# Constant products ahead of a convolution's small matmuls: a head of 128x512 and one of 128x96 before every fourth channel

## The chip, the core and the metric

The kernel runs on one core of a Trainium2 chip. The engines of that core are TensorE (PE in the rows, its weight loads PEld), VectorE (DVE), ScalarE (ACT), GpSimd (POOL) and SyncE (SP, which issues DMAs). The metric is the device time of one execution in microseconds (us), as the median of several runs. Lower is better.

## The reference

Two transformer layers run on `x` of 64 sequences by 64 positions by 128 channels, with a context of 96 channels: a cross attention, a mixture of experts, a second cross attention and a second mixture of experts, each added to `x`. Only one step of the first layer matters here. After the first attention, each of the 128 channels is convolved causally over its 64 positions with its own kernel `K` (made by an FFT in the reference), and the result is scaled and shifted:

```python
Kf = jnp.fft.rfft(K, n=n, axis=-1)
xf = jnp.fft.rfft(x, n=n, axis=1)
y = jnp.fft.irfft(xf * Kf.T[None], n=n, axis=1)[:, :L]
return y + x * D_skip
...
y = y * (1.0 + mod_gate * scale_out) + mod_gate * shift_out
xt = x_text + y
```

## The kernel before, in words

The program is a row of phases, each with its own block in which every engine has a list of instructions; at a block's end all engines meet. The phases that matter are `first_attention`, `convolution` and `first_mlp_and_router`, in this order. All data is fp32, and each fp32 matmul of the program stands in the trace as two weight loads and two matmul records.

In `convolution` a channel's convolution is a product with a 64 by 64 Toeplitz matrix. The 4096 tokens lie as 128 partitions by 32 tiles, with two sequences in a tile, one on partitions 0 to 63 and one on 64 to 127. So a channel takes two matmuls (`b2` = 0, 1), each with a 64x64 stationary matrix (`G.toe`) and 32 moving columns (`G.XM`); the two stand in opposite corners of the 128x128 array, on rows 0 to 63 and columns 0 to 63, and on rows 64 to 127 and columns 64 to 127. 16 channels (`CH`) make a group, of which there are 8 (`NG`), and a group fills one of four PSUM tiles `psy`.

The order is set by the lists and by semaphores. TensorE goes through all groups, and waits only for a PSUM tile to come free, three groups back (`y_film`). VectorE takes a finished group out of PSUM with the scale (`ym`, L1045) and adds the shift (`yn`, L1051), and GpSimd adds it to `G.XT` (L1025). SyncE loads the weights of the next phase meanwhile. ScalarE has nothing to do.

Two more constants appear in the change. `G.ones` is a 128x128 matrix of ones, and `G.pen` (128 partitions by 32 tiles by 64) holds the first attention's mask penalties, which are all zero for the masks of this case. Both are complete before the convolution begins.

Other lines that are used as measures below: in the first attention L825 (97 rows by 128 stationary columns, 512 moving), L829, L833, L834 (full or nearly full arrays, 128 moving), the weight folding's L281 and L293 (128x128 stationary) and L283 and L294 (16x128 stationary), which alternate; in the second attention L1825 and L1826 (128 stationary columns), L1831 (96x64 stationary, two side by side), L1793 (128x128 stationary, 8 moving columns) and L1863 (128x32 stationary). In the phase behind the convolution L1224 is its first transpose and L1230 its first product, both with 128x128 stationary.

Of the kernel before, what the change touches and what calls it, by code (L numbers as in the profile page):

```python
# [15 lines left out]
P = 128  # L16
B, T, D = 64, 64, 128
# [161 lines left out]
def after(eng, sem, n):  # L179

    if not isinstance(n, int) or n > 0:
        eng.wait_ge(sem, n)
# [810 lines left out]
def convolution(nc, C, A, G):  # L993


    CH = 16
    NG = D // CH
    with ExitStack() as ctx:
        psy = [C.ps(f"psy{j}", [P, CH, NT], ctx) for j in range(4)]
        ym = [C.sb(f"ym{j}", [P, NT, CH], ctx=ctx) for j in range(2)]  # L1000
        yn = [C.sb(f"yn{j}", [P, NT, CH], ctx=ctx) for j in range(2)]
        s = {n: C.sem("conv_" + n) for n in ("y", "y_film", "y_shift", "y_sum", "padded", "weights")}
        with nc.Block() as block:

            @block.sync
            def _(sp):
                sp.wait_ge(s["padded"], 1)
                m = G.mlp
                loads = ((m["w1"][:], A["L0_xattn_W1"]), (m["w2"][:], A["L0_xattn_W2"].rearrange("(c p) d -> p c d", p=P)),
                         (m["b2"][:], A["L0_xattn_b2"].partition_broadcast(P)),  # L1010
                         (m["gout"][:], A["L0_xattn_g_norm_out"].partition_broadcast(P)),
                         (m["bout"][:], A["L0_xattn_b_norm_out"].partition_broadcast(P)),
                         (m["rw1"][:], A["L0_ffn_rw1"]), (m["rw2"][:, :, 0:NE], A["L0_ffn_rw2"].rearrange("(c p) e -> p c e", p=P)),
                         (m["rb2"][:], A["L0_ffn_rb2"].partition_broadcast(P)))
                for dst, src in loads:
                    sp.dma_start(dst, src).then_inc(s["weights"], 16)
                sp.wait_ge(s["weights"], 16 * len(loads))

            @block.gpsimd
            def _(pool):  # L1020
                pool.memset(G.mlp["rw2"][:], 0.0).then_inc(s["padded"], 1)
                for g in range(NG):
                    ch = slice(g * CH, g * CH + CH)
                    pool.wait_ge(s["y_shift"], g + 1)
                    pool.tensor_tensor(G.XT[:, :, ch], G.XT[:, :, ch], yn[g % 2][:], ALU.add).then_inc(s["y_sum"], 1)  # L1025
                    pool.wait_ge(s["y_sum"], g + 1)

            @block.tensor
            def _(pe):
                for g in range(NG):  # L1030
                    after(pe, s["y_film"], g - 3)
                    for c in range(CH):
                        for b2 in range(2):
                            rows = slice(T * b2, T * b2 + T)
                            mm = pe.matmul(psy[g % 4][rows, c, :], G.toe[rows, g * CH + c, :], G.XM[rows, :, g * CH + c],
                                           start=True, stop=True)
                    mm.then_inc(s["y"], 1)

            @block.vector
            def _(dve):  # L1040
                for g in range(NG + 1):
                    if g < NG:
                        dve.wait_ge(s["y"], g + 1)
                        after(dve, s["y_shift"], g - 1)
                        dve.tensor_tensor(ym[g % 2][:], psy[g % 4][:].rearrange("p c b -> p b c"),  # L1045
                                          G.FO[:, :, g * CH:g * CH + CH], ALU.mult).then_inc(s["y_film"], 1)
                    if g > 0:
                        q = g - 1
                        dve.wait_ge(s["y_film"], q + 1)
                        after(dve, s["y_sum"], q - 1)  # L1050
                        dve.tensor_tensor(yn[q % 2][:], ym[q % 2][:], G.FO[:, :, D + q * CH:D + q * CH + CH],  # L1051
                                          ALU.add).then_inc(s["y_shift"], 1)
# [1429 lines left out]
def program(nc, A, out, last=99):  # L2482
    with ExitStack() as ctx:
# [25 lines left out]
        with ExitStack() as early:  # L2509
            G.XM = C.sb("XM", [P, NT, D], ctx=early)  # L2510
            G.FO = C.sb("FO", [P, NT, 256], ctx=early)
            G.pen = C.sb("pen", [P, NT, T], ctx=early)
            G.gin = C.sb("gin", [P, D], ctx=early)
            G.bin = C.sb("bin", [P, D], ctx=early)
            G.wq = C.sb("wq", [P, P], ctx=early)
            G.wk = C.sb("wk", [DC, P], ctx=early)
            G.wv = C.sb("wv", [DC, D], ctx=early)
            G.filmw = C.sb("filmw", [DC + 1, 512], ctx=early)
            G.toe = C.sb("toe", [P, D, T], ctx=early)
            with ExitStack() as first:  # L2520
                G.dskip, G.sign = C.sb("dskip", [P, 8], ctx=first), C.sb("sign", [P, 1], ctx=first)
                G.at0 = {n: [C.sb(f"{n}{j}", k, ctx=first) for j in range(2)] for n, k in (
                    ("kb", [P, 2, H0, T]), ("abd", [P, P]), ("at", [P, P]), ("us", [DC + 1, P]))}
                G.ring = [C.sb(f"cs{j}", [P, DC], ctx=first) for j in range(RING)]
                G.norm = {"mv": G.FO[:, NT - 5, 0:2 * NT].rearrange("p (t k) -> p t k", k=2),
                          "rstd": G.FO[:, NT - 5, 2 * NT:3 * NT], "shift": G.FO[:, NT - 5, 3 * NT:4 * NT]}
                G.kernel, G.fold = Kernel(G), Fold(C, A, G, first)
                setup(nc, C, A, G)
                C.end_phase()
                if last >= 1:  # L2530
                    first_attention(nc, C, A, G)
                    C.end_phase()
            if last >= 2:
                convolution(nc, C, A, G)
                C.end_phase()
# [49 lines left out]
```

## Time and profile before

| What | Value |
|---|---|
| Median of 3 runs | 938.84 us (936.86 to 939.61) |
| Span of the profiled execution | 935.4 us, 3.4 us under that median; what lies around the span is not in the profile |
| TensorE busy, share of the span | 710.3 us, 76% |
| VectorE busy | 673.2 us, 72% |
| Mean granted TensorE clock over the span | 0.80 of 2.4 GHz |
| The convolution's matmuls | 512 records, 259.7 to 287.3 us of the span |

A share of the span is an average over phases with different limits, so the rows of the one phase that is changed count here. The granted clock is given as a share: 1.00 is 2.4 GHz and 0.50 is 1.2 GHz. Ends of matmul records are modelled, and records overlap, so the distance between starts tells how fast TensorE goes, not the length of a record.

### The profile page before, as it was taken

The page shows a single profiled execution, that of the slowest core. Times are in us where ns is not written, and L with a number is a line of the kernel's source. Part 1 is how long each engine was busy: PE and PEld are TensorE (multiplying, and loading weights), DVE is VectorE, ACT ScalarE, POOL GpSimd, SP SyncE. Part 2 cuts the span into 40 slices and gives each one's busy share as a digit, 9 for nine tenths or more (in the row PEclk, how much of TensorE's full clock was granted, in tenths as well). Part 3 has the DMA queues.
Part 4 walks back from the last instruction along what each step waited for, and adds up shares of the span by engine and source line. Part 5 has one row for each costly group of instructions (what it writes and reads, how often), then busy time and mean ns, then how long its engine had stood idle before and what let it go on. Part 6 is the DMA issues. An engine that isn't in the chain of part 4 may idle for free. (4 is left out here: it accounts for less than half of the span.)

```text
span 935.4 us, 20537 instructions
## 1 busy us (share of the span) xinstructions
PE 710.3 (76%) x6072; PEld 508.4 (54%) x6072; DVE 673.2 (72%) x3212; ACT 473.4 (51%) x1318; POOL 564.8 (60%) x931
## 2 busy tenths in 40 slices
PE   0686898979883999972498528998888874799970
PEld 0353554545483656631275426766666652699970
DVE  6898989978524688769111167598998887699974
ACT  3566576735200455450133175577777761577740
POOL 7688877766526544210677667345777767277770
PEclk9767787957555999996599855798988885899995
DMA  6300112997213977700365330000000002698928
GB/s 143 57 25 10 41 45 64 86 88 96 40 45 140 290 250 257 243 23 0 39 115 132 88 137 1 2 4 13 25 26 25 25 28 76 216 279 264 260 69 270
DMA packets 98829, 94.41 MB, mean 101 GB/s; under 512 B 37511, under 2 KB 82302, under 8 KB 98142
## 3 DMA queue, kind: packets, MB, share of 16 engines
q1 hardware_dynamic: 91268, 79.34, 33.1%
q0 software_dynamic: 6592, 13.58, 6.0%
q8 instruction: 50, 0.82, 0.4%
q14 instruction: 61, 0.50, 0.3%
q10 hardware_dynamic: 858, 0.17, 0.1%
HBM read 47.76 MB, written 43.19 MB: 97 GB/s over the span
## 5 line engine op out<-in xcount | busy, mean ns | idle before, releaser
L2402 POOL DMA_INDIRECT expert_pairs<-e_ys,e_home x78 | 75.4, 967 | 38.4 <-issue 23.5
L1742 POOL TENSOR_SCALAR a_kb<-a_kr,a_m,a_bk 128x128 f32<-128x128 f32 x128 | 57.9, 452 | 44.4 <-ACT a_kr L1981 32.3
L1760 POOL DMA_INDIRECT expert_slots<-r_rows,r_slotu x64 | 63.3, 989 | 30.3 <-DVE r_rows L2136 15.1
L950 DVE MATCH_REPLACE8 work<-m,work 128x64 f32<-128x64 f32 x384 | 75.7, 207 | 0.0
L1484 POOL DMA_INDIRECT ex_rows<-rows,slot_source x32 | 30.7, 960 | 52.7 <-POOLq L1163 43.2
L937 DVE MAX8 m<-work 128x8 f32<-128x64 f32 x384 | 57.0, 209 | 0.0
L825 PE MATMUL psf<-filmw,us 97*128 97x512 f32 x64 | 51.6, 902 | 3.0 <-ACT FO L846 2.9
L1815 PE MATMUL a_pss<-a_kb,a_qt 32*64 32x256 f32 x512 | 41.5, 463 | 13.9 <-ACT a_pp L1966 11.7
L2168 DVE TENSOR_REDUCE a_mx<-a_pss 128x8 f32<-128x512 f32 x64 | 43.9, 686 | 8.1 <-PE a_pss L1815 7.8
L2369 PE MATMUL e_ps<-e_XH,e_wh 128*128 128x256 f32 x156 | 48.1, 308 | 1.5 <-DVE e_XL L2414 1.5
L1536 ACT ACTIVATE ex_hs<-ex_psh,vec 128x512 f32<-128x512 f32 x32 | 22.0, 687 | 51.2 <-PE ex_psh L1517 50.5
L2371 PE MATMUL e_ps<-e_XH,e_wl 128*128 128x256 f32 x156 | 44.6, 286 | 0.0
L2370 PE MATMUL e_ps<-e_XL,e_wh 128*128 128x256 f32 x156 | 44.6, 286 | 0.0
L1961 ACT ACTIVATE a_pp<-a_dd 128x512 f32<-128x512 f32 x32 | 20.2, 631 | 45.1 <-DVE a_dd L2177 45.1
L1890 PE MATMUL a_psp<-ident,a_pp 128*128 128x128 f32 x256 | 39.5, 306 | 1.9 <-ACT a_pt L2014 1.9
L2219 DVE RECIPROCAL a_rt<-a_pso 128x128 f32<-128x128 f32 x31 | 29.5, 951 | 14.8 <-PE a_pso L1882 11.9
L1309 ACT ACTIVATE rt_rs<-mlp_psh,vec 128x512 f32<-128x512 f32 x32 | 22.0, 687 | 34.7 <-PE mlp_psh L1267 34.7
L203 POOL TENSOR_SCALAR mlp_ln_v<-mlp_ln_mv 128x4 f32<-128x4 f32 x24 | 5.5, 229 | 54.0 <-DVE mlp_ln_mv L195 54.0
L1494 POOL DMA_INDIRECT planes<-ex_ys,slot_home x32 | 31.2, 976 | 10.9 <-issue 9.1
L2177 DVE TENSOR_TENSOR a_dd<-a_mx,a_pss 128x512 f32<-128x512 f32 x64 | 35.5, 554 | 2.2
L808 PE MATMUL pss<-kb,qt 128*64 128x256 f32 x128 | 28.9, 541 | 10.7 <-ACT kb L846 10.7
L2014 ACT ACTIVATE a_pt<-a_psp 128x512 f32<-128x512 f32 x64 | 35.4, 611 | 2.2 <-PE a_psp L1890 2.0
(464 smaller groups left out, 2418.2 us busy)
## 6 DMA issues: line engine op xcount, KB each, us to landing
expert_slots<-rt_unfilled SPq DMA_DIRECT2D x151, 130.0 KB, 2.6
ahead<-folded_weights SPq DMA_DIRECT2D x20, 386.0 KB
e_wf<-folded_weights SPq DMA_DIRECT2D x19, 386.0 KB, 4.2
planes<-rt_zeros SPq DMA_DIRECT2D x4, 1024.0 KB
ew<-in_L_ffn_ew SPq DMA_DIRECT2D x16, 256.0 KB, 4.0
pair_y<-expert_pairs SPq DMA_DIRECT2D x16, 256.0 KB, 5.6
e_xr<-expert_slots SPq DMA_DIRECT2D x27, 130.0 KB, 3.3
folded_weights<-fold_done SPq DMA_DIRECT2D x8, 384.0 KB, 4.3
```

Source lines behind the costliest of these rows:

```text
L825: pe.matmul(psf[:], us[j][:], G.filmw[:], start=True, stop=True).then_inc(s["film"], 1)
L937: mx = dve.max(m8[x.j][:, h, r, :], src[:, h, :])
L950: return own.did(dve.match_replace(wk_[x.j][:, h, :], m8[x.j][:, h, r, :], src[:, h, :], TAKEN))
L1742: m = pool.tensor_scalar(kb[a.j][:, :, h, :], k, m4[:, h:h + 1], bk4[:, h:h + 1], ALU.mult, ALU.add)
L1760: pool.indirect_dma_start(G.slots, bass.IndirectOffsetOnAxis(ap=slot[:, b, k, t:t + 1], axis=0), rb[b % NB][:, k, t, :], None).then_inc(se ...
L1815: mm = pe.matmul(pss[half][T * b:T * b + T, h, 0:HG * T], qt[g.j][rows, T * b:T * b + T], kb[g.j][rows, b, :, :], start=True, stop=True)
L1890: mm = pe.transpose(psp[half][:, k, :], pp[x.j][:, h:h + 2, :].rearrange("p h k -> p (h k)"), G.ident[:])
L2168: dve.tensor_reduce(m, scores(half), AX.X, ALU.min).then_inc(s["lowest"], 1)
L2369: pe.matmul(psh[m][c][:], wh[j][:, m, c, :], XH[j][:], start=True, stop=False)
L2370: pe.matmul(psh[m][c][:], wh[j][:, m, c, :], XL[j][:], start=False, stop=False)
L2371: pe.matmul(psh[m][c][:], wl[j][:, m, c, :], XH[j][:], start=False, stop=True).then_inc(h_ps[m][c], 1)
L2402: pool.indirect_dma_start(G.pair, bass.IndirectOffsetOnAxis(ap=home[i % NY][:, k:k + 1], axis=0), ys[i % NY][:, k, :], None).then_inc(kept ...
```

## The change

TensorE's list of `convolution` gets one matmul of 512 columns at its start, and one of 96 columns ahead of every fourth channel, 32 of them in all. Each has `G.ones` as stationary matrix (128x128) and the first columns of `G.pen` as moving ones, and writes a PSUM tile of its own, `psw`, that nothing reads. They have no semaphore, neither to wait for nor to raise. No instruction of another engine changes.

```diff
@@ -997,6 +997,8 @@
     NG = D // CH
     with ExitStack() as ctx:
         psy = [C.ps(f"psy{j}", [P, CH, NT], ctx) for j in range(4)]
+        psw = C.ps("conv_warm", [P, 512], ctx)
+        held = G.pen[:, 0:512 // T, :].rearrange("p n t -> p (n t)")
         ym = [C.sb(f"ym{j}", [P, NT, CH], ctx=ctx) for j in range(2)]
@@ -1027,9 +1029,12 @@
 
             @block.tensor
             def _(pe):
+                pe.matmul(psw[:], G.ones[:], held, start=True, stop=True)
                 for g in range(NG):
                     after(pe, s["y_film"], g - 3)
                     for c in range(CH):
+                        if c % 4 == 0:
+                            pe.matmul(psw[:, 0:96], G.ones[:], held[:, 0:96], start=True, stop=True)
                         for b2 in range(2):
                             rows = slice(T * b2, T * b2 + T)
                             mm = pe.matmul(psy[g % 4][rows, c, :], G.toe[rows, g * CH + c, :], G.XM[rows, :, g * CH + c],
```

TensorE's list at the seam of the first attention and the convolution, before (an x counts equal instructions of the program, out<-in are tiles, and the shape is that of the result):

```order
L825 MATMUL psf<-filmw,us 128x512
L637 UNCONDITIONAL_BRANCH
L1028 UNCONDITIONAL_BRANCH
L1035 MATMUL psy<-XM,toe 64x32 x256
L1003 UNCONDITIONAL_BRANCH
```

All 256 matmuls of the convolution stood in one run of one shape. The same place in the changed list (`conv_warm` is `psw`; the line numbers are those of the changed kernel):

```order
L825 MATMUL psf<-filmw,us 128x512
L637 UNCONDITIONAL_BRANCH
L1030 UNCONDITIONAL_BRANCH
L1032 MATMUL conv_warm<-pen,ones 128x512
L1037 MATMUL conv_warm<-pen,ones 128x96
L1040 MATMUL psy<-XM,toe 64x32 x8
```

The last two rows then repeat to the end of the phase, 32 times in all: one product over the full array, then eight on its quarters.

## Rows read from the trace of the kernel before

**Rows 1.** Groups of instructions, 259 to 293 us: count | busy us, mean ns | idle before, releaser

```profile
L1035 PE MATMUL psy<-XM,toe 64*64 64x32 f32 x512 | 27.5, 291 | 2.3 <-PEq L637 2.3
L1035 PEld LDWEIGHTS psy<-XM,toe 64*64 64x64 f32 x512 | 27.4, 223 | 3.9 <-issue 3.9
...
L1045 DVE TENSOR_TENSOR ym<-psy,FO 128x512 f32<-128x512 f32 x8 | 5.5, 692 | 30.0 <-PE psy L1035 30.0
```

**Rows 2.** Timeline at the convolution's end: start us, us, instruction, idle before and releaser

```profile
287.29 0.69 DVE L1045 TENSOR_TENSOR ym<-psy,FO 128x512 f32<-128x512 f32 x1 [2.12 <-PE psy L1035]
287.90 1.28 DVE L1051 TENSOR_TENSOR yn<-ym,FO 128x512 f32<-128x512 f32 x2
288.73 2.89 POOL L1025 TENSOR_TENSOR XT<-XT,yn 128x512 f32<-128x512 f32 x2 [2.16 <-DVE yn L1051]
292.09 1.28 ACT L1289 ACT_TABLE_LOAD   x1 [34.01 <-PEq L1003]
```

**Rows 3.** TensorE by stretch: stretch, its length, busy us, granted clock, DMA share, GB/s

```profile
259.70:287.30 27.60, 27.52 (x512) 0.50 0.15 39
...
292.10:303.60 11.50, 1.11 (x4) 0.50 0.65 273
303.60:307.00 3.40, 3.38 (x7) 0.50 0.98 396
307.00:310.00 3.00, 3.00 (x14) 1.00 1.07 315
229.00:237.00 8.00, 8.00 (x26) 0.50 0.95 113
221.90:225.00 3.10, 3.10 (x17) 1.00 0.43 48
586.00:592.00 6.00, 6.00 (x57) 0.50 0.00 0
602.00:605.00 3.00, 3.00 (x64) 1.00 0.02 5
```

**Rows 4.** TensorE's timeline, 228 to 237 us

```profile
228.72 1.06 PE L825 MATMUL psf<-filmw,us 97*128 97x512 f32 x1
229.58 0.64 PE L829 MATMUL psb<-abd,cs 128*96 128x128 f32 x2
230.00 0.63 PE L833 MATMUL psa<-xf,wq 128*128 128x128 f32 x2
230.43 0.63 PE L834 MATMUL psa<-cf,wk 96*128 96x128 f32 x2
...
231.46 0.79 PE L283 MATMUL side<-fold_bt,fold_ar 16*128 16x128 f32 x2
232.18 0.80 PE L281 MATMUL side<-ident,fold_wr 128*128 128x128 f32 x2
232.91 0.79 PE L283 MATMUL side<-fold_bt,fold_ar 16*128 16x128 f32 x2
```

**Rows 5.** TensorE's timeline, 588 to 592 us

```profile
588.03 0.80 PE L1825 MATMUL a_psx<-XF,a_wq 128*128 128x128 f32 x2
588.62 0.63 PE L1826 MATMUL a_psx<-ctxT,a_wk 96*128 96x128 f32 x2
589.18 0.70 PE L1831 MATMUL a_psx<-a_wv,ctxT 96*64 96x64 f32 x8
589.81 1.88 PE L1793 MATMUL a_pso<-e_wgt,XF 128*128 128x8 f32 x8
591.61 0.66 PE L1863 MATMUL a_pso<-a_pt,a_vb 128*32 128x64 f32 x16
```

**Rows 6.** TensorE's timeline, 222 to 225 us, at the full clock

```profile
222.06 0.49 PE L293 MATMUL side<-ident,fold_w2r 128*128 128x128 f32 x2
222.47 0.48 PE L294 MATMUL side<-fold_bt,fold_a 16*128 16x128 f32 x2
...
224.01 1.02 PE L825 MATMUL psf<-filmw,us 97*128 97x512 f32 x2
224.87 0.38 PE L829 MATMUL psb<-abd,cs 128*96 128x128 f32 x2
```

**Rows 7.** TensorE's timeline, 603 to 604 us, at the full clock

```profile
603.08 0.45 PE L1831 MATMUL a_psx<-a_wv,ctxT 96*64 96x64 f32 x8
603.46 1.06 PE L1793 MATMUL a_pso<-e_wgt,XF 128*128 128x8 f32 x8
```

**Rows 8.** TensorE's timeline behind the convolution

```profile
303.62 1.11 PE L1224 MATMUL mlp_pst<-ident,mlp_xs 128*128 128x128 f32 x4 [3.93 <-DVE mlp_xs L211]
304.52 4.83 PE L1230 MATMUL mlp_psh<-mlp_xf,mlp_w 128*128 128x512 f32 x8
```

## The prediction, as it was put on record

> **What bounds the kernel now.** I read the groups of instructions in the convolution first, then the end of that phase in the timeline, then the table by stretch for the clock, and last those places where TensorE changes between shapes. The first view shows who waits. VectorE was idle for 30.0 us ahead of its eight evictions, each time for TensorE, and TensorE's 512 records wait for nothing but the phase's start [rows 1]. So in this phase TensorE's own list is the bound. The end of the phase shows that nothing else covers it: the last eviction, the shift and GpSimd's addition follow the last group one behind the other, and the next phase starts at 292.09 us, when ScalarE has waited 34 us for it [rows 2]. Whatever TensorE's list gains or loses between 259.7 and 287.3 us moves the end of the phase, and with it the kernel's end, by as much.
>
> The clock was at 0.50, the 1.2 GHz level, in all of those 27.6 us, although TensorE was busy for 27.52 of them [rows 3]. 512 records in 27.3 us make 0.0533 us a record, or 0.107 us for the two that stand in opposite corners of the array. The kernel's phases before and behind are at either level.
>
> **What the change adds.** Nothing is removed or waited for, and no DMA or other engine is touched. There are 33 more products on TensorE, each of two records, and each of another shape than its neighbours: 128x128 stationary among 64x64 ones. I cost them at the 1.2 GHz level and ask about the clock afterwards.
>
> *Columns.* A record of 512 columns takes 0.86 us from L825's start to that of L829 at 1.2 GHz, so 1.67 ns a column [rows 4]. The head is two of these, 1.7 us. An inserted product of 96 columns is two records of 0.16 us, 0.32 us.
>
> *Change of shape.* The trace of before has this too. L833 to L834 is a pair of 128-column records between neighbours of the same shape: 0.43 us. L283 and L281, of the same column count but with 16 stationary rows and 128 in turn, take 0.72 to 0.73 us a pair, with nothing between them that waits [rows 4]. So 0.29 us goes to a pair for which the shape changes on the way in and on the way out. L1825 shows the way in alone: it comes from another shape, is followed by its own shape, and takes 0.59 us, 0.16 over 0.43; the way out is then the other 0.13 [rows 5]. For 96 columns I take 32 columns off the last record, 0.05 us: **0.67 us an inserted product**. If both records were shorter by that it would be 0.62; with nothing off it is 0.72.
>
> The Trainium skill says why this is so ("TensorEngine Tiling (Array Packing)", section Key Properties): changing the tiling mode, and not only the tile, drains TensorE. It gives no price. This trace agrees, with 0.13 to 0.16 us at each change, and by columns alone, as if there were no drain, the same sum would be 11.9 us.
>
> *The eight small products behind it.* They too now start from a change and end in one. L1831 is the nearest row: 8 records with 64-wide stationary matrices, two side by side, between two 128-wide shapes. It takes 0.63 us [rows 5]. Four pairs at the convolution's 0.107 us are 0.43, so 0.20 us is over. L1831 has 64 moving columns and the convolution 32, whose records finish 0.05 us sooner behind the last load, so I take 0.15. The other bound is L1793, 8 records with 8 columns each, which do almost nothing but load: 1.80 us [rows 5] against 8 x 0.215 (half the unchanged pair's 0.43), 0.08 over. **0.15 us a block**, from 0.08 to 0.20.
>
> Sum: 32 x (0.67 + 0.15) = 26.2 us, and the head 1.7, together 27.9 us. The phase's 27.3 us of matmuls become 55.2. The bounds are 32 x (0.62 + 0.08) + 1.7 = 24.1 us, and 32 x (0.72 + 0.20) + 1.9 = 31.3 us (the head's own load left open, as L1825's 0.16, in the second). No cover exists: TensorE is what all wait for here. The profiled execution's span goes from 935.4 to 963.3, and with the 3.4 us by which the median stands over that span, **966.7 us**.
>
> *The clock.* I take it to stay at 0.50. It rose at 307 us: ahead of that TensorE had run L1224 and L1230, all 128x128 stationary, with 512 columns each in the latter and no pause from 303.62 us on (7 records in 3.40 us, 3.38 busy) [rows 3, 8]. The head has two records of that kind, and then come changes of shape. Those ran in 229 to 237 us: TensorE was busy 8.00 of 8.00 us with full-array products and 16-row ones in turn, and the clock stayed at 0.50 [rows 3, 4]. That stretch is the nearest row to the changed phase. Behind the phase nothing changes either: TensorE has 1.11 us of work in the 11.5 us from 292.1 on [rows 3], so a clock won in the convolution would be lost before L1230.
>
> **Rivals.**
>
> *A: the changes of shape are free here.* Then only columns count: 32 x 0.32 + 1.7 = 11.9 us, 950.7 us. For it: weight loads overlap matmuls all through the convolution (PEld is busy 27.4 us beside PE's 27.5) [rows 1]. Against it: at each change of shape that I found, there is a price. The Trainium skill has the rule behind this rival ("TensorE: Matmul & The Clock Gate", Step-by-step, step 1): the next tile's weights load while this tile's matmul runs; L833 and L834 agree with it and L281 with L283 do not.
>
> *B: the clock rises to 2.4 GHz behind the head and stays.* The convolution's own 27.3 us would halve to 13.65. At that level a switched pair takes 0.41 us (L293 to L294), a column 0.84 ns (L825 to L829, 0.86 us for two records), so an insertion is 0.41 - 0.03 = 0.38 [rows 6]; L1831's block takes 0.38, against 4 x 0.0533 = 0.21, so 0.17 - 0.03 = 0.14 over [rows 7]. 32 x 0.52 + 13.65 + 1.7 = 32.0 us, 4.7 us more than now: 943.5 us. Even a raised clock does not pay for the changes of shape. If it rose for a part of the phase, the time would lie between this and the forecast.
>
> The Trainium skill speaks for a rise ("TensorE: Matmul & The Clock Gate", Part 1): the slow clock is the default, and activity releases it. The rise at 307 us agrees; the 27.5 busy microseconds at 0.50 in the convolution show that not every kind of activity does.
>
> *C, the other side: the clock rises and the inserted loads hide under the small products.* Then 13.65 + 32 x 0.16 + 1.7 = 20.5 us, 6.8 less than now: 932.0 us. The point that decides is the price of an insertion at 2.4 GHz: under (27.3 - 13.65 - 1.7) / 32 = 0.37 us the change wins. The rows give 0.52, of which 0.16 is columns.
>
> *D: no difference.* It would take a clock that rises for all of the phase and an insertion of 0.37 us, so it lies between B and C.
>
> **How the numbers follow.** The forecast has 0.86, A 0.04, B or a part of it 0.05, C 0.03, D 0.02. About 0.3%, 2.8 us, is what a measurement of this kernel tells from no change. The forecast's bounds are 938.84 + 24.1 = 962.9 and 938.84 + 31.3 = 970.1; the runs of before spread over 2.75 us, which I put on either side: 960 to 973 us. That holds nearly all of the forecast's 0.86, so 8 in 10. Slower has the forecast, A and B, 0.95; faster C, 0.03; the same D, 0.02.
>
> **What would show it.** Right: 578 records (512, and 66 of the new lines) in some 55 us; the clock at 0.50 from the phase's start to its end; from one inserted product's start to the next 1.67 us (16 x 0.0533 + 0.82); VectorE's wait for TensorE in this phase up from 30.0 to about 58 us; all later phases as long as before. Wrong in the price of a change: a step of 1.17 us at 0.50. Wrong in the clock: 1.00 within the phase, and steps of 0.95 us or less. Wrong elsewhere: a difference that lies behind 292 us of the old time, in a phase that the change does not touch.

## The result

The changed kernel takes 966.88 us (median of 4 runs, 966.74 to 968.44), the kernel before 939.21 us (4 runs). The ratio is 1.0333, with a 95% interval of 1.0284 to 1.0381: slower by 27.7 us. Ratios and intervals are the record's, taken over the executions that it counts as fast, while medians are over all; here the ratio of the two medians is 1.0295. The prediction was 966.7 us.

The page of the changed kernel, its first part and the granted clock by slice:

```profile
PE 743.3 (77%) x6138; PEld 531.7 (55%) x6138; DVE 673.9 (70%) x3212; ACT 473.7 (49%) x1318; POOL 564.8 (58%) x931
...
PEclk9786777856555599998679955599888886899995
```

TensorE has 66 records more, two for each of the 33 products, and 33 us more busy time (710.3 before); the other engines have what they had, within 0.7 us. A higher busy share of TensorE is here a longer kernel. The groups of the convolution, which answer to [rows 1]:

```profile
L1040 PE MATMUL psy<-XM,toe 64*64 64x32 f32 x512 | 34.1, 294 | 0.0
...
L1037 PE MATMUL conv_warm<-pen,ones 128*128 128x96 f32 x64 | 23.5, 472 | 0.0
...
L1050 DVE TENSOR_TENSOR ym<-psy,FO 128x512 f32<-128x512 f32 x8 | 5.5, 692 | 57.6 <-PE psy L1040 57.6
```

VectorE's wait for TensorE went from 30.0 to 57.6 us. Its own work is the same 5.5 us. TensorE in the phase by stretch, and around the next phase's first products, as in [rows 3]; the first row is of all engines (PE, PEld, DVE, ACT, POOL), the others of TensorE alone:

```profile
263.78:318.90 55.12, 55.08 (x578) 46.43 (x578) 8.42 (x13) 0.00 (x0) 7.74 (x7) 0.50 0.08 20
...
323.70:335.20 11.50, 1.11 (x4) 0.50 0.65 273
335.20:338.70 3.50, 3.48 (x8) 0.50 0.98 385
338.70:341.70 3.00, 3.00 (x14) 1.00 1.00 297
```

The clock stayed at 0.50 through all 55.1 us, and rose where it rose before, behind L1224 and L1230 (now L1229 and L1235). TensorE's timeline near the end of the phase, and what follows it, which answers to [rows 2]:

```profile
315.46 0.74 PE L1037 MATMUL conv_warm<-pen,ones 128*128 128x96 f32 x2
316.13 1.07 PE L1040 MATMUL psy<-XM,toe 64*64 64x32 f32 x16
317.13 0.74 PE L1037 MATMUL conv_warm<-pen,ones 128*128 128x96 f32 x2
317.80 1.07 PE L1040 MATMUL psy<-XM,toe 64*64 64x32 f32 x16
...
318.92 0.69 DVE L1050 TENSOR_TENSOR ym<-psy,FO 128x512 f32<-128x512 f32 x1 [5.38 <-PE psy L1040]
...
323.72 1.28 ACT L1294 ACT_TABLE_LOAD   x1 [61.59 <-PEq L1005]
```

The distance between starts is what counts: 0.67 us from an inserted product to the small ones, 1.00 us on to the next inserted product.

Where the time went, by the two profiled executions. From the phase's first matmul record to the start of the last eviction it was 287.29 - 259.73 = 27.56 us, and is now 318.92 - 263.78 = 55.14 us: 27.58 us more. From there to the end of the span it was 648.1 us and is 648.3. The span itself grew by 31.8 us, since the phase also began 4.05 us later. That part lies in the first attention, which the change does not touch, and it is a matter of which executions were profiled: that of the changed kernel was the slowest of its four (968.44 us, a span of 967.2; the other spans are 965.5 to 965.7), and that of before was a quick one. In all four a time is 1.2 us over its span, so of the 3.4 us by which the span of before lies under its median, some 2 us say only that.

### The profile page after: what moved, and what is told of

Read it like the earlier page. It is cut to its first block and busy times, and to the rows that moved or that the text cites. A ratio compares the mean times of both kernels' runs of the same rounds, so it can differ in the third digit from the quotient of the medians.

```text
span 967.2 us, 20669 instructions
## 1 busy us (share of the span) xinstructions
PE 743.3 (77%) x6138; PEld 531.7 (55%) x6138; DVE 673.9 (70%) x3212; ACT 473.7 (49%) x1318; POOL 564.8 (58%) x931
## 5 line engine op out<-in xcount | busy, mean ns | idle before, releaser
L825 PE MATMUL psf<-filmw,us 97*128 97x512 f32 x64 | 52.0, 908 | 3.0 <-ACT FO L846 2.9
L1050 DVE TENSOR_TENSOR ym<-psy,FO 128x512 f32<-128x512 f32 x8 | 5.5, 692 | 57.6 <-PE psy L1040 57.6
L2224 DVE RECIPROCAL a_rt<-a_pso 128x128 f32<-128x128 f32 x31 | 29.5, 950 | 14.9 <-PE a_pso L1887 12.0
L1027 POOL TENSOR_TENSOR XT<-XT,yn 128x512 f32<-128x512 f32 x8 | 10.4, 1298 | 48.9 <-DVE yn L1056 48.8
L741 POOL TENSOR_TENSOR sc<-dd,pen 128x256 f32<-128x256 f32 x32 | 23.2, 724 | 26.5 <-ACT dd L846 26.5
```

What stands on the lines that cost most here:

```text
L825: pe.matmul(psf[:], us[j][:], G.filmw[:], start=True, stop=True).then_inc(s["film"], 1)
```

## The experiments

The theory: each inserted product has a price of its own, columns plus two changes of shape, at a clock that stays at 1.2 GHz. Rivals, with the prediction's letters: the clock decides (B, C), the price is not that of the shape (A, or the foreign weights as such), or the price depends on how the products stand.

Most runs are a single execution. The kernel's whole time varies from execution to execution by more than these prices, mostly ahead of the convolution (see the end), so the runs are compared by **the phase**: from its first matmul record to the start of the last eviction, 27.56 us before and 55.14 us after.

**Head alone** (e1).

```diff
-                        if c % 4 == 0:
-                            pe.matmul(psw[:, 0:96], G.ones[:], held[:, 0:96], start=True, stop=True)
```

> Only the head of 512 columns stays, the 32 inserted products go. Measured from the first convolution-phase matmul to the start of the last eviction (before 27.6 us, changed kernel 55.1). Theory (columns and changes of shape at the 1.2 GHz level): 27.6 + 1.7 + 0.15 = 29.4 us, granted clock 0.50 throughout. Rival (the head raises the clock): part of the phase at 1.00 and a phase under 28 us, down to 15.4.

Measured: phase 29.54 us, clock 0.50 throughout, the kernel 942.88 us. The head raises nothing, and costs 1.98 us. That is 0.13 more than the 1.85 expected. In the changed kernel the head takes 1.84 us from its start to the first inserted product (263.78 to 265.62 us), not 1.7. The likely reason, which no run tests, is that its first load has no matmul to lie under: the second record starts 1.00 us behind the first, and the inserted product 0.84 us behind the second.

**No head** (e2).

```diff
-                pe.matmul(psw[:], G.ones[:], held, start=True, stop=True)
```

> The 32 inserted products stay, the head goes. Theory: 27.6 + 32 x 0.82 = 53.8 us for the phase, a step of 1.67 us from one inserted product to the next, clock 0.50. Rival (the head sets the clock for what follows): the phase differs from 55.1 by something other than the head's 1.7 us of columns less one change of shape, 1.2 to 1.7 us.

Measured: phase 53.42 us, 962.43 us in all, clock 0.50. TensorE's timeline in it:

```profile
300.52 1.07 PE L1039 MATMUL psy<-XM,toe 64*64 64x32 f32 x16
301.52 0.74 PE L1036 MATMUL conv_warm<-pen,ones 128*128 128x96 f32 x2
302.19 1.07 PE L1039 MATMUL psy<-XM,toe 64*64 64x32 f32 x16
```

The step is 1.67 us again, so the head has no influence on the rest. The two parts nearly add: 1.98 and 25.86 us alone, 27.84, against 27.58 together, where the first inserted product has the head's shape and needs no change.

**The same columns without a change of shape** (e3).

```diff
                         if c % 4 == 0:
-                            pe.matmul(psw[:, 0:96], G.ones[:], held[:, 0:96], start=True, stop=True)
+                            for b2 in range(2):
+                                rows = slice(T * b2, T * b2 + T)
+                                pe.matmul(psw[rows, 0:96], G.ones[rows, 0:T], held[rows, 0:96], start=True, stop=True)
```

> Each inserted product of 96 columns over the full array becomes two of 96 columns with 64x64 stationary matrices, in the two corners that the convolution itself uses; the head stays. The same number of columns streams, but the shape does not change. Theory (the price is the change of shape): a step of 0.85 + 0.32 = 1.17 us, phase 27.6 + 32 x 0.32 + 1.9 = 39.7 us. Rival (the price is that other weights come in between, whatever their shape): a step of 1.4 us or more, phase over 47 us.

Measured: phase 39.78 us, 943.59 us in all. The timeline:

```profile
279.75 0.56 PE L1039 MATMUL conv_warm<-pen,ones 64*64 64x96 f32 x4
280.10 1.01 PE L1042 MATMUL psy<-XM,toe 64*64 64x32 f32 x16
280.92 0.56 PE L1039 MATMUL conv_warm<-pen,ones 64*64 64x96 f32 x4
```

A step of 1.17 us where the full-array product makes 1.67. The same 96 columns twice, foreign weights too, but the array keeps its shape: 0.50 us less each time. So it is not the foreign weights, and columns explain 0.32 of 0.82 us; the other 0.50 goes with the shape. The shape brings a second difference, though: a full-array product loads 128 weight columns each time, and these load 64. The run with two copies (e5, below) tells the two apart.

**A quarter of them** (e4) and **twice as many in the same places** (e5).

```diff
-                        if c % 4 == 0:
+                        if c == 0:
```

> The full-array product of 96 columns stands ahead of every sixteenth channel, 8 in all instead of 32; the head stays. Theory (a fixed price for each): 27.6 + 8 x 0.82 + 1.7 = 35.8 us for the phase, clock 0.50. Rival (what they cost depends on how close they stand): a price for each that is not 0.82 us by more than 0.1.

```diff
-                            pe.matmul(psw[:, 0:96], G.ones[:], held[:, 0:96], start=True, stop=True)
+                            for k in range(2):
+                                pe.matmul(psw[:, 0:96], G.ones[:], held[:, 0:96], start=True, stop=True)
```

> Each inserted product of 96 columns over the full array is issued twice in a row; the head stays. Theory: the second copy finds the array in its own shape, so it costs columns only, 0.32 us, or its two weight loads of 128 columns where these are longer, 0.43 us (the unchanged pair's row): a step of 1.99 to 2.10 us, phase 65 to 69 us. Rival (each product pays its own entry and exit): a step of 2.3 us or more, phase over 76 us.

Measured: 35.61 us and 68.78 us; 953.81 and 978.73 us in all. With e4 the price of one is (35.61 - 29.54) / 8 = 0.76 us, with one of the eight spared its entry. In e5 a second copy adds (68.78 - 55.14) / 32 = 0.43 us, the row of a pair that keeps its shape [rows 4], and not 0.82. The timeline of e5:

```profile
301.24 1.17 PE L1038 MATMUL conv_warm<-pen,ones 128*128 128x96 f32 x4
302.33 1.07 PE L1041 MATMUL psy<-XM,toe 64*64 64x32 f32 x16
303.33 1.17 PE L1038 MATMUL conv_warm<-pen,ones 128*128 128x96 f32 x4
```

So most of the 0.50 us is paid per change, not per product. The two runs together split it: a full-array product behind its like costs 0.43 us, 0.11 over the 0.32 of its columns, and about 0.39 us is left for the two changes of shape. (The 0.11 would be its longer loads, as expected ahead of the run; that a load costs as much between two changes was not tried.)

**A head that does raise the clock, with the inserted products** (e6).

```diff
-                pe.matmul(psw[:], G.ones[:], held, start=True, stop=True)
+                for k in range(8):
+                    pe.matmul(psw[:], G.ones[:], held, start=True, stop=True)
```

> The head of 512 columns is issued eight times in a row (about 13.6 us at 1.2 GHz, half of that at 2.4), the 32 inserted products stay. It asks for the price of an insertion at the full clock. Theory: the clock rises during the head, as it rose behind the phase in the kernel before; while it is at 1.00 a step takes 0.95 us (rival B's price). Whether it stays there is open: if it did, the convolution behind the head would take 30 us. Rival C: a step of 0.60 us at 1.00.

Measured: phase 56.06 us, 957.34 us in all. TensorE by stretch, and two steps of its timeline at the full clock:

```profile
251.60:255.30 3.70, 3.62 (x5) 0.50 0.00 0
255.30:260.70 5.40, 5.40 (x15) 1.00 0.65 180
260.70:269.00 8.30, 8.30 (x159) 1.00 0.04 6
269.00:308.00 39.00, 38.69 (x424) 0.50 0.01 2
```

```profile
264.26 0.46 PE L1038 MATMUL conv_warm<-pen,ones 128*128 128x96 f32 x2
264.66 0.66 PE L1041 MATMUL psy<-XM,toe 64*64 64x32 f32 x16
265.25 0.46 PE L1038 MATMUL conv_warm<-pen,ones 128*128 128x96 f32 x2
```

The clock rose in the head, and fell to 0.50 at 269 us, in the middle of the pattern of the change, with TensorE busy 8.30 of 8.30 us. At 1.00 a step takes 0.98 to 0.99 us. Rival B had 0.95, rival C 0.60.

**The same head with no inserted products** (e7).

```diff
-                pe.matmul(psw[:], G.ones[:], held, start=True, stop=True)
+                for k in range(8):
+                    pe.matmul(psw[:], G.ones[:], held, start=True, stop=True)
...
-                        if c % 4 == 0:
-                            pe.matmul(psw[:, 0:96], G.ones[:], held[:, 0:96], start=True, stop=True)
```

> The head of 512 columns eight times, no inserted products. It asks what the small products do to a clock that is up. Theory (they do not hold it, as they did not raise it): the clock is at 1.00 during the head, then falls to 0.50; the convolution behind the head takes 27.6 us less half of its part at 1.00, 24 to 27 us. Rival (they hold it): 13.7 us at 1.00.

```profile
252.60:256.30 3.70, 3.70 (x5) 0.50 0.00 0
256.30:261.40 5.10, 5.10 (x13) 1.00 0.69 190
261.40:276.70 15.30, 15.18 (x513) 1.00 0.03 7
```

Here the theory missed and its rival was right. The small products do not raise the clock, but they held it at 1.00 for 15.3 us. The phase took 24.43 us, with 8.9 us of head in it; the convolution itself ran in 14.9 us up to its last record. (Of the whole time, 926.95 us, most of the difference lies ahead of the phase, which began at 252.6 us.)

**Long head with insertions that keep the shape** (e11). It is e6 with e3's insertion.

> The head eight times, and the inserted products as pairs of 64x64 stationary matrices in the convolution's own corners, 96 columns each, so without a change of shape. In the run with eight heads and full-array insertions the clock fell again 8 us into the convolution, in the one without insertions it did not. Theory (the changes of shape bring it down): 1.00 to the phase's end, a step of 0.47 + 0.16 = 0.63 us, 20 us behind the head. Rival (any product put between brings it down): a fall to 0.50 within the phase and steps of 1.17 us behind it.

```profile
267.70:273.40 5.70, 5.65 (x7) 0.50 0.27 85
273.40:298.00 24.60, 24.60 (x650) 1.00 0.10 25
```

Measured: phase 30.30 us, 947.56 us in all, a step of 0.63 us (as from 279.07 to 279.70 us in its timeline), and the clock at 1.00 to the end. Against e6 only the shape of the inserted products differs. So it is the full-array insertions, with the changes of shape that they bring, that lowered a raised clock; small products alone (e7) or with company of their own shape held it. Each of these is one execution.

**Company in the two idle corners** (e8). No head, no full-array products.

```diff
-                pe.matmul(psw[:], G.ones[:], held, start=True, stop=True)
...
-                        if c % 4 == 0:
-                            pe.matmul(psw[:, 0:96], G.ones[:], held[:, 0:96], start=True, stop=True)
+                        for b2 in range(2):
+                            rows, over = slice(T * b2, T * b2 + T), slice(T - T * b2, 2 * T - T * b2)
+                            pe.matmul(psw[over, 0:64], G.ones[rows, 0:T], held[rows, 0:64], start=True, stop=True)
```

> No head and no full-array products. Beside each of the convolution's matmuls stands one more product of constants, 64x64 stationary and 64 columns, in the two corners of the array that the convolution leaves idle, so that no change of shape occurs and four corners work. Open whether the four run side by side and whether the clock rises. If they run side by side at 0.50: phase 27.6 us or a little over. If the clock rises as well: 14 to 18 us, and the kernel is faster by 10 to 13 us. If they run one behind the other: 55 us.

```profile
260.50:263.60 3.10, 3.09 (x118) 0.51 0.02 5
263.60:270.40 6.80, 4.43 (x284) 1.00 0.61 150
270.40:273.80 3.40, 3.01 (x118) 0.50 0.02 5
273.80:280.60 6.80, 3.85 (x244) 1.00 0.02 5
```

Measured: phase 28.76 us, not 14 to 18, and 940.53 us in all. The four corners run side by side (118 records in 3.1 us, against 58 at the convolution's own pace), and the clock rises. But at 1.00 TensorE is busy for only 4.43 of 6.80 us: in the phase it stood six times with nothing that the profile shows it to wait for, 7.6 us in all, and the clock fell again, at 270.4 and at 280.6 us. The gain was lost there.

**A short head, without insertions, timed** (e9, e10, e12; 12 executions each, 29 of the kernel before on the same chip, one of which, 3259.73 us, is far from all others). In e9 the head is issued four times. In e10 and e12 the products stand at the end of the first attention's list instead, where TensorE waits for the phase's end, four and three of them (into a PSUM tile of that phase that is no longer read):

```diff
                 march(slot, -3, NT + 3)
+                held = G.pen[:, 0:512 // T, :].rearrange("p n t -> p (n t)")
+                pe.wait_ge(s["side_kept"], 13 + 3 * (NE - 1))
+                for k in range(3):
+                    pe.matmul(side[:], G.ones[:], held, start=True, stop=True)
```

> The head of 512 columns four times at the phase's start, no inserted products. In the run with eight and no insertions the clock rose 3.7 us into the head, and the convolution ran at 1.00 to its end in 15 us. Theory (the small products hold a clock that is up; full-array products without a change of shape raise it): the clock rises during the four, the head takes 5 to 7 us, the convolution 15, the phase 20.5 to 22.5 us instead of 27.6, the kernel 932 to 934 us. Rival (the rise needs the eight): clock 0.50 and a phase of 34.5 us, 946 us.

> The four products of 512 columns stand at the end of the first attention's list for TensorE, in which it otherwise waits 2.3 us for the phase's end, and no product stands in the convolution. Theory: 2.3 us of the head lie under that wait; from the old start of the convolution's matmuls to the last eviction 18 to 20 us, the kernel 929 to 931 us. Rival (the pause between the two phases lets the clock fall): more than 30 us, 942 us or over.

> As with four products at the end of the first attention's list, with three. Theory: if the three suffice to raise the clock, one product less, 0.9 to 1.7 us faster than with four, or the same where the convolution runs its first part at 0.50 in its place. Rival (three are too few): 0.50 to the end, 27.6 us and 2.8 us more, 942 us.

| Run | Median, us | Ratio to the kernel before | 95% interval |
|---|---|---|---|
| before, same chip | 937.75 | | |
| e9, head of four | 934.30 | 0.9948 | 0.9906 to 0.9991 |
| e10, four early | 931.97 | 0.9935 | 0.9895 to 0.9975 |
| e12, three early | 929.91 | 0.9949 | 0.9917 to 0.9981 |

All three beat the kernel before by these ratios, by 0.5 to 0.65%; those of the medians are 0.9963, 0.9938 and 0.9916. It is a small gain, and which of them is best the intervals don't tell. e9's median is 0.3 us over its expected range, e10's 1 us. In the profiled executions less was won than expected: e9's phase is 27.94 us, not 20.5 to 22.5 and not under the 27.56 of before, so its phase does not show where its 0.5% comes from. The theory of e9 and e10, that the small products hold a raised clock to the end, failed. TensorE's timelines of e9 and e12, and e12's table by stretch:

```profile
254.42 5.07 PE L1033 MATMUL conv_warm<-pen,ones 128*128 128x512 f32 x8 [2.35 <-PEq L637]
259.42 5.96 PE L1039 MATMUL psy<-XM,toe 64*64 64x32 f32 x197
266.25 16.07 PE L1039 MATMUL psy<-XM,toe 64*64 64x32 f32 x315 [0.87 <-issue]
```

```profile
254.11 4.64 PE L845 MATMUL side<-pen,ones 128*128 128x512 f32 x6
259.05 9.73 PE L1039 MATMUL psy<-XM,toe 64*64 64x32 f32 x327 [0.30 <-PEq L637]
269.68 8.57 PE L1039 MATMUL psy<-XM,toe 64*64 64x32 f32 x185 [0.90 <-issue]
```

```profile
254.10:257.90 3.80, 3.80 (x6) 0.50 0.00 0
257.90:271.60 13.70, 12.50 (x395) 1.00 0.31 77
271.60:278.30 6.70, 6.65 (x127) 0.50 0.02 4
```

Three products were enough to raise the clock. Some 10 us into the convolution TensorE paused for 0.90 us, and behind the pause the clock fell. From the last L825 to the last eviction e12 has 26.0 us (252.27 to 278.29), the kernel before 31.95 (255.34 to 287.29): 5.9 us won. In e10 (pause 1.22 us) it is 3.9 us, in e9 (pause 0.87 us, fall at 267.5 us) nothing. e7 and e11 had no such pause within the small products, and no fall. That the pause brings the clock down fits these five. It does not hold for every pause: in e8 the clock stayed at 1.00 for 4 us behind one of 1.04 us (276.49 to 280.6 us), and fell behind the next.

What causes the pauses was not tried, but where they stand points at the supply of instructions. Counted from the first product of the head, e9's pause stands behind 205 records of TensorE (8 + 197), e10's and e12's behind 333 (8 + 325, 6 + 327), which is 128 more; in e8, which has no head, all six stand behind 205 records of the phase or a multiple of 128 more. In the DMA packets of these traces, the queue named "instruction" moves 16 KB about once per 128 of TensorE's records, and every one of these pauses ends 2.2 to 2.9 us behind the start of such a packet. In e7 the packets came every 3.7 us, and there was no pause. In e10 and e12 the one ahead of the pause came 6.4 and 6.0 us behind the one before it, while the next phase's weights were arriving; e7's weights had come under its long head (DMA share 0.03 beside the small products, against 0.31 in e12's stretch at 1.00).

## Why the prediction was right, point by point

- *TensorE's list is the bound of the phase.* 27.58 us more on TensorE in the phase became 27.7 us of the median. VectorE's wait is 57.6 us (about 58 forecast), and from the last eviction to the end the difference is 0.2 us.
- *An inserted product takes 0.67 us.* Measured 0.67 (317.13 to 317.80 us). The price was read from L281 and L283, which change only the row count, and it held for a change of rows and columns at once.
- *The small products behind it take 0.15 us more.* Measured 1.00 us a block, less 16 x 0.0533 = 0.85: 0.15. Together with the entry above, a step of 1.67 us, as forecast. The rows had put 0.29 and 0.15 us on the changes, with 0.05 off for the fewer columns; that makes 0.39, which is what e5 leaves for them.
- *The head costs 1.7 us.* Alone 1.98, mis-sized by 0.13 us for its open load. With the first insertion behind it, which needs no change, it was made up: 266.13 - 263.78 = 2.35 us for both, against 1.7 + 0.67 = 2.37 in the sum.
- *The clock stays at 0.50.* It did, in the changed kernel and in e1 to e5. The picture chosen for it, products of changing shape at 0.50, is also what lowered a raised clock in e6.
- *Rival A* (no price for the shape) is refuted by the step: 1.67 us, not 1.17. Its arithmetic is right where the shape does not change (e3: 1.17). The Trainium skill says ("TensorEngine Tiling (Array Packing)", section Key Properties) that changing the tiling mode drains TensorE. The steps with and without a change, 1.67 and 1.17 us, agree with it.
- *Rival B.* Its price for a step at the full clock was 0.95 us, and e6 measured 0.98 to 0.99. The difference is in the small products: they take 0.058 us a pair at 1.00 (14.9 us for 256 pairs in e7), not half of 0.107. What it assumed besides, a clock that stays, fails with the insertions.
- *Rival C* fell with the same step: 0.98 against the 0.60 that it needed.

One reading of the prediction needs a limit. That the convolution ran at 0.50 shows that its products do not raise the clock; the expectation for e7 took it to mean also that they do not hold it, and that was wrong.

By the prediction's other sum, against the profiled execution's own span, 963.3 us stood against 967.2. The missing 4 us are the late start of the phase, not a term of the sum.

That the forecast met the median to 0.2 us is in part luck. The phase came out 0.3 us under the sum, the median of before moved by 0.4 us with its fourth execution, and the ratio's interval is as wide as 4.5 us to either side. What the runs confirm is the price per step.

## What to carry to other kernels

Before putting work on an engine to keep it busy, look for who waits for it: here every added microsecond was the kernel's. A product of another shape cost TensorE more for its shape (0.50 us at 1.2 GHz, about 0.39 of it for the two changes) than for its columns (0.32 us), so work that is to fill or to warm should have the shape of its neighbours, or stand in one piece where TensorE waits anyway. Whether work raises a clock and whether it holds one are two questions, and each asks for a run of its own.

## What was not expected of the hardware

A stream of 64x64 products ran 27.5 us at 0.50 without raising the clock, and 15.3 us at 1.00 without losing it. What differed was what stood ahead of it.

At the full clock, long streams of such small products stopped for up to 2.2 us with no wait that the profile shows, at places that lie 128 records or a multiple of that apart in TensorE's list (e8, e9, e10, e12).

The time at which the convolution begins varied from 251.7 to 267.8 us between profiled executions, though nothing ahead of it differs in those two (e6 and e11, on two chips; on one chip e3 and e4 began at 253.1 and 265.7). TensorE's rows from 60 to 250 us, in e6 and then in e11:

```profile
60.00:250.00 190.00, 159.13 (x630) 0.78 0.52 58
```

```profile
60.00:250.00 190.00, 165.56 (x622) 0.72 0.44 56
```

The granted clock is 0.78 and 0.72. In the first attention it is now at one level and now at the other [rows 3], and differently in each execution. It does not settle the start by itself: e9 has 0.72 in the same stretch and began at 254.4 us. What lies ahead of the convolution is most of the kernel's spread, some 16 us, while from the last eviction to the end all profiled executions take 647.9 to 651.6 us; this is the reason for comparing phases.
